# Gate values as two rows spread over the partitions through DRAM, and half of the depthwise convolution on TensorE, in a mixer and mixture-of-experts block

## The chip, the cores and the metric

One core of one Trainium2 chip (trn2) runs the kernel. The metric is the device time of one execution in microseconds (us), median of several runs. The profile is of one execution. TensorE is PE (its weight loads are PEld), VectorE is DVE, ScalarE is ACT, GpSimd is POOL, SyncE is SP.

## The reference, cut to what matters

x has 32 sequences of 256 tokens of width 128. It is normalised, and two branches are added to it: a gated linear recurrence ("mixer") and a mixture of 8 experts with the top 2 of each token.

```python
xn = layernorm(x)
xz = xn @ W_in.T                      # 128 -> 2 x 256
x_proj, z = split(xz)
x_conv = silu(causal_depthwise_conv(x_proj, conv_w, 4 taps) + conv_b)   # per channel, per sequence
x_ssm = x_conv @ W_x.T                # 16 columns Bm, 16 columns Cm, 256 columns dt_in
dt = softplus(dt_in @ W_dt.T + b_dt)
alpha = sigmoid(0.1 * dt)
B_gate = sigmoid(mean(Bm))            # one value per token
C_gate = sigmoid(mean(Cm))            # one value per token
h = scan(clip(alpha, .01, .99), (1 - alpha) * B_gate * x_conv)
y = (h * C_gate + D * x_conv) * silu(z)
out = x + y @ W_out.T + experts(xn)
```

## The kernel before, in words

Channels lie on the partitions (256 of them in two halves, c = 0 and 1) and tokens in the free dimension. A group is 512 tokens, two sequences; there are 16 groups. The program has five stages:

- Setup: x is loaded and normalised, transposed into `xnT`, weights are transposed and folded, the top 2 experts of each token are chosen and each token's row in the expert buffer `moe_in` (DRAM) is worked out.
- Stage A, mixer steps g = 0 to 11. In step g, PE projects and convolves group g+1 and computes for group g; ACT and DVE finish group g-1. At the same time POOL writes token rows to `moe_in` with 128 indirect DMAs (L558), held back by `follow` (L532) to places in DVE's chain.
- Experts: 36 tiles of up to 512 token slots, each with two products, a gate, and a product down (L784 to L841), with inputs loaded by SP. POOL writes the results to `moe_out` (DRAM) with 142 indirect DMAs (L572).
- Steps 12 to 16 of the mixer.
- Sums: as soon as all expert results are written, POOL adds `moe_out` onto `xacc` or the output with 16 accumulating DMAs of 512 KB (L586), blocks 6 and 7 first; SP stores what is finished (L469 to L478).

Each engine's program is written out by hand, in the order of its queue, and semaphores tie the engines. Within one mixer step:

- PE (`mix`, L707): `convolved(g)` (needs the taps of the last step, `s_taps`), `out` (the product with W_out, needs `y2` of DVE), `project` (dt, needs `s_xc` and `s_dt`), `gated` (z), `gates`. `convolved` (L693) projects channel half 1 of both sequences (L694), half 0 of the second sequence (L695), and for half 0 of the first sequence does the convolution itself as four products with pre-scaled weights `Wtap` (L697).
- `gates` (L650) multiplies with `WgB`, whose 128 columns are all equal, so that the mean of Bm (and of Cm) comes out on all 128 partitions: 2 gates x 2 halves of K.
- ACT (`mix`, L988): the first tap with its bias (`acc`, L995 and L1001), silu of the part convolved on PE (L1000), `decay` (tanh `th` L1009, `al` L1015), then a table load (L1025), abs, exp and ln of the softplus (L1030 to L1036), a table load (L1037), silu of z (L1040), tanh of the gates into `thg` (L1044), silu of the rest of the convolution (L1048).
- DVE (`mix`, L1322): taps 1 to 3 (`tap`, L1297: for each, half 0 of the second sequence and half 1 of both), `add_out` (L1319), and the chain: `gbuf` (L1251), clip (L1254), times B gate (L1260), scan (L1266), times C gate (L1271), plus D x (L1277), times silu(z) to `y2` (L1283), and softplus (L1293).
- SP (L418 to L451): when the tables are ready, 8 padding fills of `moe_in` of 266 KB (L420), then stores of finished blocks (`store_base`, L426), then, after `s_xp` 12 and `s_z` 12, the weights of expert tiles 0 and 1 (six DMAs of 128 KB, L436 to L443), then, after all 128 scatters (L444), the rows of tiles 0 and 1 (`xs`, L446).

At the handoff to the experts PE waits for the gates' activation and transposes the rows of tile 0:

```python
            pe.wait_ge(s_thg, STEPS_A)
            transp(0, 0, 0, True)
```

Of the kernel before, what the change touches and what calls it, by code (L numbers as in the profile page):

```python
# [12 lines left out]
P = 128  # L13
# [3 lines left out]
GROUP = 512  # L17
# [43 lines left out]
def block_kernel(nc, x, W_in, conv_w, conv_b, W_x, W_dt, b_dt, A_log, D_skip, W_out,  # L61
                 w_gate, w1, w3, w2, out):
    xs_dram = nc.dram_tensor("moe_in", (EXPERTS * REGION, ROW), F32, kind="Internal").ap()
    yt_dram = nc.dram_tensor("moe_out", (PAIRS, D), F32, kind="Internal").ap()

    ctx = ExitStack()
    with ctx:
# [16 lines left out]
        WgB = sb("WgB", [P, 4, P])  # L84
# [33 lines left out]
        thg = sb("thg", [P, SLOT3, 2, GROUP])  # L118

# [120 lines left out]
        s_tap0 = sem("s_tap0")  # L240
        s_taps = sem("s_taps")
# [11 lines left out]
        s_thg = sem("s_thg")  # L253
        s_ch = sem("s_ch")
# [92 lines left out]
        def _(sp):  # L347
# [70 lines left out]
            sp.wait_ge(s_eid, 1)  # L418
            sp.wait_ge(s_zrow, 1)
            for e in range(EXPERTS):  # L420
# [3 lines left out]
            sp.wait_ge(s_fill, 16 * EXPERTS)  # L424
# [10 lines left out]
            first = []  # L435
            for t in range(2):  # L436
                e = entry(eid_i, t, EXPERTS - 1)
                first.append(entry(src_i, t, EXPERTS * REGION - SLOTS))
# [154 lines left out]
        def _(pe):  # L593
# [56 lines left out]
            def gates(g, slot, b):  # L650
                static = isinstance(g, int)
                if not (static and g < 1):
                    pe.wait_ge(s_thg, g)
# [53 lines left out]
            def mix(g, slot, a, b, c, d):  # L707
                static = isinstance(g, int)
                if a and not (static and g == STEPS_A):
                    if not (static and g + 1 < 1):  # L710
                        pe.wait_ge(s_taps, g + 1)
                    if static and g == 0:
                        pe.wait_ge(s_xc, 1)
                    convolved(g)
                if d:
                    out(g, slot, b)
                if b:
                    project(g, slot, b)
                if a:
# [5 lines left out]
                if b:  # L725
                    if static and g == STEPS_A:
                        pe.wait_ge(s_yc, MOE_TILES)
                    gates(g, slot, b)
# [55 lines left out]
            def up(t, b, first):  # L784
# [3 lines left out]
                for m, (ps, free, done) in enumerate(((PA, s_sil, s_h1), (PB, s_hid, s_h3))):  # L788
                    if not first:
                        pe.wait_ge(free, t)  # L790
                    elif m == 0:
                        pe.wait_ge(s_taps, STEPS_A + 1)
                    else:
# [49 lines left out]
            pe.wait_ge(s_thg, STEPS_A)  # L843
# [47 lines left out]
        def _(act):  # L891
            act.preload_act_table_set("natural_log_exp_and_others")
            def setup(r):
# [7 lines left out]
                elif r == 1:  # L901
# [3 lines left out]
                    act.activation(WgB[:, :, :], PB[:, 512:1024].rearrange("p (a b) -> p a b", a=4),  # L905
# [30 lines left out]
            def take(g):  # L936
# [36 lines left out]
            act.activation(acc[:, 1, :], PA[:, GROUP:2 * GROUP], ACT.Identity, bias=cb[:, 1:2], scale=cw[:, 1, TAPS - 1:TAPS])  # L973
            act.wait_ge(s_xp, 1)
            act.activation(acc[:, 0, SEQ:GROUP], PA[:, SEQ:GROUP], ACT.Identity,
                           bias=cb[:, 0:1], scale=cw[:, 0, TAPS - 1:TAPS]).then_inc(s_tap0, 1)
# [3 lines left out]
            setup(2)  # L980
            act.wait_ge(s_taps, 1)
            act.activation(xc[:, 0, 0, 0:SEQ], PA[:, 0:SEQ], ACT.Silu, bias=cb[:, 0:1])
            act.activation(xc[:, 0].rearrange("p a b -> p (a b)")[:, SEQ:2 * GROUP], flat(acc[:, :, :])[:, SEQ:2 * GROUP],
                           ACT.Silu).then_inc(s_xc, 1)
# [3 lines left out]
            def mix(g, slot, a, b, c, d, held=False):  # L988
                static = isinstance(g, int)
                nxt = (slot + 1) % SLOT3  # L990
                def conv():
                    act.wait_ge(s_xr, g + 2)
                    if not (static and g + 1 < 1):
                        act.wait_ge(s_xc, g + 1)
                    act.activation(acc[:, 1, :], PA[:, GROUP:2 * GROUP], ACT.Identity,  # L995
                                   bias=cb[:, 1:2], scale=cw[:, 1, TAPS - 1:TAPS])
# [3 lines left out]
                    act.activation(xc[:, nxt, 0, 0:SEQ], PA[:, 0:SEQ], ACT.Silu, bias=cb[:, 0:1])  # L1000
                    act.activation(acc[:, 0, SEQ:GROUP], PA[:, SEQ:GROUP], ACT.Identity,  # L1001
                                   bias=cb[:, 0:1], scale=cw[:, 0, TAPS - 1:TAPS]).then_inc(s_tap0, 1)
# [20 lines left out]
                if b:  # L1023
# [13 lines left out]
                    act.preload_act_table_set("silu_and_others")  # L1037
                if a and not held:
                    act.wait_ge(s_z, g + 2)
                    act.activation(sz[:, nxt].rearrange("p a b -> p (a b)"), PB[:, :], ACT.Silu).then_inc(s_sz, 1)  # L1040
                if b:

                    act.wait_ge(s_g, g + 1)
                    act.activation(thg[:, slot].rearrange("p a b -> p (a b)"), PD[:, :], ACT.Tanh,  # L1044
                                   scale=0.5).then_inc(s_thg, 1)
                if a and not held:
                    act.wait_ge(s_taps, g + 2)
                    act.activation(xc[:, nxt].rearrange("p a b -> p (a b)")[:, SEQ:2 * GROUP], flat(acc[:, :, :])[:, SEQ:2 * GROUP],  # L1048
                                   ACT.Silu).then_inc(s_xc, 1)
# [44 lines left out]
            def tile_step(t, n, b, more):  # L1094
# [6 lines left out]
                if more:  # L1101
# [10 lines left out]
            act.activation(xc[:, STEPS_A % SLOT3].rearrange("p a b -> p (a b)")[:, SEQ:2 * GROUP], flat(acc[:, :, :])[:, SEQ:2 * GROUP],  # L1112
                           ACT.Silu).then_inc(s_xc, 1)
# [24 lines left out]
        def _(ve):  # L1138
# [98 lines left out]
            def chain(g, slot, part):  # L1237
# [17 lines left out]
                elif part == 1:  # L1255
# [3 lines left out]
                    ve.wait_ge(s_thg, g)  # L1259
# [37 lines left out]
            def tap(g, j, c_):  # L1297

                if c_ == 0:
                    if j == 1:  # L1300
                        ve.wait_ge(s_tap0, g + 2)
                    else:
                        ve.wait_ge(s_cv, g * 2 + j + 1)
                own = slice(1 - c_, SPG)
                a_v = acc[:, c_, :].rearrange("p (s l) -> p s l", s=SPG)[:, own, j:SEQ]
                p_v = PA[:, c_ * GROUP:(c_ + 1) * GROUP].rearrange("p (s l) -> p s l", s=SPG)[:, own]
                ins = ve.scalar_tensor_tensor(a_v, p_v[:, :, 0:SEQ - j], cw[:, c_, TAPS - 1 - j:TAPS - j],  # L1307
                                              a_v, ALU.mult, ALU.add)
                if c_ == HALVES - 1:
                    ins.then_inc(s_taps if j == TAPS - 1 else s_cv, 1)  # L1310
# [11 lines left out]
            def mix(g, slot, a, b, c, d):  # L1322

                if a:
                    tap(g, 1, 0)
                    tap(g, 1, 1)
# [4 lines left out]
                if a:  # L1331
                    tap(g, 2, 0)
                    tap(g, 2, 1)
                if c:
                    chain(g, slot, 1)
                if a:
                    tap(g, 3, 0)
                    tap(g, 3, 1)
# [7 lines left out]
            def mix_before_experts(g, slot, a, b, c, d):  # L1346


                tap(g, 1, 0)
                tap(g, 1, 1)  # L1350
                add_out(g)
                chain(g, slot, 0)
                for j in (2, 3):
                    tap(g, j, 0)
                    tap(g, j, 1)
# [202 lines left out]
            tap(g, 1, 0)  # L1558
            tap(g, 1, 1)
# [3 lines left out]
            tap(g, 2, 0)  # L1563
            tap(g, 2, 1)
            chain(g, slot, 1)
            tap(g, 3, 0)
            tap(g, 3, 1)
# [9 lines left out]
            tap(g, 1, 0)  # L1577
            tap(g, 1, 1)
            add_out(g)
            chain(g, slot, 0)  # L1580
            tap(g, 2, 0)
            tap(g, 2, 1)
            chain(g, slot, 1)
            tap(g, 3, 0)
            tap(g, 3, 1)
# [55 lines left out]
```

## Time and profile before

| what | value |
|---|---|
| time, median of 3 runs | 488.89 us (488.41 to 489.1) |
| the profiled execution's own time | 488.94 us |
| its span, first to last instruction | 487.0 us |
| busy: PE, DVE, ACT, POOL | 436.2, 410.7, 311.3, 319.6 us |
| DMA traffic | 62.75 MB, 129 GB/s in the mean |
| mean granted clock of PE | 0.974 of full speed |

A share of the span is a mean over stages with different limits, so the rows below are taken stage by stage: what an engine did, and what ended the wait before it ("idle before <- releaser").

### The profile page before, as it was taken

How to read it: one execution, taken by the hardware profiler on the slowest of the kernel's cores; microseconds unless marked ns; L12 is line 12 of the kernel's file. 1: busy time of each engine (PE TensorE's matmuls, PEld its weight loads, DVE VectorE, ACT ScalarE, POOL GpSimd, SP SyncE). 2: the span in 40 equal slices, each digit the busy share in tenths (PEclk: the TensorE clock that was granted, in tenths of full speed). 3: DMA queues.
4: the chain of work that ended last, by engine and by line, in shares of the span. 5: the costliest groups of instructions: out<-in, count | busy, mean ns of one | idle time of the engine just before them, and what ended most of it. 6: DMA issues, size and time to landing. Idle time of an engine off the chain costs nothing. (4 is left out here: it accounts for less than half of the span.)

```text
span 487.0 us, 8269 instructions
## 1 busy us (share of the span) xinstructions
PE 436.2 (90%) x2188; PEld 319.0 (66%) x2188; DVE 410.7 (84%) x868; ACT 311.3 (64%) x421; POOL 319.6 (66%) x345
## 2 busy tenths in 40 slices
PE   0989959899999999998999999999999999999743
PEld 0877525555555555554788888989888999555332
DVE  5999986999999999996997676767777786998993
ACT  2785657888998888898544444444443555698830
POOL 3647777777777777671077777777777777745210
PEclk9999988999999999999999999999999999999876
DMA  9601139122121312132667776666665652039997
GB/s 246 178 3 46 56 101 172 53 66 74 45 93 45 94 45 65 57 111 62 165 190 227 218 219 172 199 179 184 176 186 155 194 173 75 10 50 176 200 212 184
DMA packets 70939, 62.75 MB, mean 129 GB/s; under 512 B 9034, under 2 KB 63214, under 8 KB 70912
## 3 DMA queue, kind: packets, MB, share of 16 engines
q1 hardware_dynamic: 57728, 35.37, 28.0%
q0 software_dynamic: 10944, 25.52, 20.0%
q10 hardware_dynamic: 2240, 1.57, 1.0%
q8 instruction: 9, 0.15, 0.1%
q14 instruction: 18, 0.15, 0.1%
HBM read 38.94 MB, written 29.64 MB: 141 GB/s over the span
## 5 line engine op out<-in xcount | busy, mean ns | idle before, releaser
L572 POOL DMA_INDIRECT moe_out<-xnT,dst_u x142 | 145.5, 1025 | 64.3 <-issue 32.3
L558 POOL DMA_INDIRECT moe_in<-xn,slot_u x128 | 141.5, 1106 | 46.2 <-issue 35.7
L1092 ACT ACTIVATE xn<-PA 128x1024 f32<-128x1024 f32 (+1 forms) x36 | 36.6, 1016 | 61.0 <-PE PA L803 52.3
L1447 DVE TENSOR_TENSOR xn<-xn,PB 128x1024 f32<-128x1024 f32 (+1 forms) x36 | 43.4, 1206 | 33.2 <-PE PB L803 29.3
L837 PE MATMUL PD<-xnT,xn 128*128 128x128 f32 x536 | 65.7, 275 | 0.0
L837 PEld LDWEIGHTS PD<-xnT,xn 128*128 128x128 f32 x536 | 62.8, 192 | 0.0
L685 PE MATMUL PC<-xc,Wc 128*128 128x512 f32 x128 | 59.3, 607 | 2.9 <-DVE ebuf L1293 2.9
L1307 DVE SCALAR_TENSOR_TENSOR acc<-PA,cw,acc 128x255 f32<-128x255 f32 (+2 forms) x96 | 54.2, 606 | 8.2 <-ACT acc L1001 8.1
L658 PE MATMUL PD<-xc,WgB 128*128 128x512 f32 x128 | 57.5, 592 | 0.0
L658 PEld LDWEIGHTS PD<-xc,WgB 128*128 128x128 f32 x128 | 24.2, 190 | 30.1 <-issue 30.1
L672 PE MATMUL PB<-WoT,y 128*128 128x128 f32 x240 | 32.2, 290 | 12.0 <-DVE y L1283 12.0
L685 PEld LDWEIGHTS PC<-xc,Wc 128*128 128x128 f32 x128 | 23.8, 195 | 27.8 <-issue 24.1
L672 PEld LDWEIGHTS PB<-WoT,y 128*128 128x128 f32 x240 | 29.7, 201 | 17.7 <-DVE y L1283 17.2
L1266 DVE TENSOR_TENSOR_SCAN hbuf<-al,gbuf 128x512 f32<-128x512 f32 x32 | 37.3, 1208 | 0.1
L1086 ACT ACTIVATE xhi<-PD 128x512 fp32r<-128x512 f32 (+1 forms) x36 | 21.2, 590 | 24.2 <-PE PD L781 24.2
L697 PE MATMUL PA<-xnT,Wtap 128*128 (+4 forms) x128 | 31.1, 387 | 0.0
L703 PE MATMUL PB<-xnT,WinT 128*128 (+1 forms) x64 | 30.2, 594 | 1.0 <-ACT bdt L912 1.0
L1508 DVE TENSOR_TENSOR xnT<-PD,slot_p 128x512 f32<-128x512 f32 (+1 forms) x36 | 24.6, 683 | 5.9 <-PE PD L837 5.2
L1060 ACT ACTIVATE whi<-xnT 128x512 fp32r<-128x512 f32 x36 | 22.6, 628 | 9.1 <-issue 7.2
L1009 ACT ACTIVATE th<-ebuf,bdt 128x512 f32<-128x512 f32 x32 | 21.3, 714 | 10.8 <-DVE ebuf L1293 10.8
L799 PE MATMUL PA<-xhi,whi 128*128 128x512 f32 x62 | 26.9, 434 | 1.5 <-DVE wlo L1453 0.7
L1030 ACT ACTIVATE ebuf<-PC,bdt 128x512 f32<-128x512 f32 x32 | 20.2, 683 | 11.6 <-PE PC L685 11.6
(211 smaller groups left out, 941.1 us busy)
## 6 DMA issues: line engine op xcount, KB each, us to landing
xnT<-in_L_ffn_w_dram SPq DMA_DIRECT2D x108, 128.0 KB
xn<-moe_in SPq DMA_DIRECT2D x31, 266.0 KB
out_dram<-moe_out POOLq DMA_DIRECT2D x10, 512.0 KB, 15.2
out_dram<-xacc SPq DMA_DIRECT2D x7, 512.0 KB, 3.5
xacc<-moe_out POOLq DMA_DIRECT2D x6, 512.0 KB, 6.7
moe_out<-xnT,dst_u POOLq DMA_INDIRECT x142
moe_in<-zrow SPq DMA_DIRECT2D x8, 266.0 KB, 6.5
moe_in<-xn,slot_u POOLq DMA_INDIRECT x128, 2.4
```

What stands on the lines that cost most here:

```text
L558: gp.indirect_dma_start(xs_dram, bass.IndirectOffsetOnAxis(ap=slot_u[:, k, j:j + 1], axis=0), xn_row[:, j, :], None).then_inc(s_scat, 16)
L572: gp.indirect_dma_start(yt_dram, bass.IndirectOffsetOnAxis(ap=dst_u[:, t, j:j + 1], axis=0), yo[t % OUTS][:, j, :], None, bounds_check=PAI ...
L658: last = pe.matmul(PD[:, n * GROUP:(n + 1) * GROUP], WgB[:, n * 2 + k, :], xc[:, slot, k, :], start=(k == 0), stop=(k == 1))
L672: last = pe.matmul(PB[:, j * D:(j + 1) * D], y2[:, k, j * P:(j + 1) * P], WoT[:, k, :], start=(k == 0), stop=(k == 1))
L685: last = pe.matmul(PC[:, c_ * GROUP:(c_ + 1) * GROUP], Wc[:, k, c_ * P:(c_ + 1) * P], xc[:, slot, k, :], start=(k == 0), stop=(k == 1))
L697: last = pe.matmul(PA[:, j:SEQ], Wtap[:, TAPS - 1 - j, :], source(g, 0, SEQ - j), start=(j == 0), stop=(j == TAPS - 1))
L703: last = pe.matmul(PB[:, c_ * GROUP:(c_ + 1) * GROUP], WinT[:, INNER + c_ * P:INNER + (c_ + 1) * P], source(g), start=True, stop=True)
L837: last = pe.matmul(PD[:, 512 + j * D:512 + (j + 1) * D], hid[b][:, k * SLOTS + j * P:k * SLOTS + (j + 1) * P], (w2x[t - FULL] if mixed and ...
L1092: act.activation(halves(sil, t), halves(PA[:, :], t), ACT.Silu).then_inc(s_sil, 1)
L1266: last = ve.tensor_tensor_scan(hbuf[:, c_, :], al[:, c_, :], gbuf[:, c_, :], 0.0, ALU.mult, ALU.add)
L1307: ins = ve.scalar_tensor_tensor(a_v, p_v[:, :, 0:SEQ - j], cw[:, c_, TAPS - 1 - j:TAPS - j], a_v, ALU.mult, ALU.add)
L1447: ve.tensor_tensor(halves(hid[b], t), halves(sil, t), halves(PB[:, :], t), ALU.mult).then_inc(s_hid, 1)
```

## The change

- `WgB` (128 equal columns) becomes `WgR` with two columns, one for each gate. `gates` then needs two products instead of four and yields two rows of 512 values, on partitions 0 and 1. ACT's tanh works on these two rows (`gt`).
- A new function on SP, `spread_gates(g)`, writes `gt` (4 KB) to the DRAM tensor `gate_rows`, waits until it is written, and reads the row of 1024 values back 128 times, onto every partition of `thg` (512 KB).
- All four taps of channel half 0, of both sequences, are done on PE (`Wtap`); L695, the second `acc` activation and the DVE taps of half 0 go.
- On PE `gates` comes ahead of `gated`; on ACT the tanh of the gates ahead of silu(z).
- On SP the eight fills are no longer one burst: each follows a `spread_gates`, and the stores are put between them. The loads for expert tiles 0 and 1 come behind `spread_gates(11)`. `spread_gates(12)` to `(15)` come behind the expert loads and ahead of the stores.

```diff
+            def spread_gates(g):
+                sp.wait_ge(s_gt, g + 1)
+                if g >= 1:
+                    sp.wait_ge(s_thg, g * 16)
+                if g >= 3:
+                    sp.wait_ge(s_ch, (g - 3) * CHAIN + 6)
+                row = gt_dram[g % SLOT3:g % SLOT3 + 1, :]
+                sp.dma_start(row.rearrange("o (n l) -> (o n) l", n=2), gt[:, :]).then_inc(s_gw, 16)
+                sp.wait_ge(s_gw, (g + 1) * 16)
+                sp.dma_start(thg[:, g % SLOT3].rearrange("p n l -> p (n l)"),
+                             row.broadcast_to([P, 2 * GROUP])).then_inc(s_thg, 16)
...
-            for k in range(STORED - 1):
-                store_base(k)
+            for g in range(STEPS_A - 1):
+                if g >= 4 and g % 2 == 0 and g // 2 - 2 < STORED - 1:
+                    store_base(g // 2 - 2)
+                spread_gates(g)
+                if g < EXPERTS:
+                    fill(g)
+            e01 = [entry(eid_i, t, EXPERTS - 1) for t in range(2)]
+            first = [entry(src_i, t, EXPERTS * REGION - SLOTS) for t in range(2)]
+            spread_gates(STEPS_A - 1)
             sp.wait_ge(s_xp, 12)
             sp.wait_ge(s_z, 12)
...
+            sp.wait_ge(s_fill, 16 * EXPERTS)
             sp.wait_ge(s_scat, 16 * TOP_K * TILES)
...
+            for g in range(STEPS_A, GROUPS):
+                spread_gates(g)
 
             for k in STORES:
...
-                for n in range(2):
-                    for k in range(HALVES):
-                        last = pe.matmul(PD[:, n * GROUP:(n + 1) * GROUP], WgB[:, n * 2 + k, :],
-                                         xc[:, slot, k, :], start=(k == 0), stop=(k == 1))
+                for k in range(HALVES):
+                    last = pe.matmul(PD[0:2, 0:GROUP], WgR[:, k, :], xc[:, slot, k, :], start=(k == 0), stop=(k == 1))
...
-                pe.matmul(PA[:, SEQ:GROUP], WinT[:, 0:P], source(g, SEQ, SEQ), start=True, stop=True)
+                if not (isinstance(g, int) and g + 1 < 1):
+                    pe.wait_ge(s_xq, g + 1)
+                own = PA[:, 0:GROUP].rearrange("p (s l) -> p s l", s=SPG)
+                rows = source(g).rearrange("p (s l) -> p s l", s=SPG)
                 for j in range(TAPS):
-                    last = pe.matmul(PA[:, j:SEQ], Wtap[:, TAPS - 1 - j, :], source(g, 0, SEQ - j),
+                    last = pe.matmul(own[:, :, j:SEQ], Wtap[:, TAPS - 1 - j, :], rows[:, :, 0:SEQ - j],
                                      start=(j == 0), stop=(j == TAPS - 1))
...
-            pe.wait_ge(s_thg, STEPS_A)
+            pe.wait_ge(s_gt, STEPS_A)
...
+                    act.wait_ge(s_g, g + 1)
+                    if not (static and g < 1):
+                        act.wait_ge(s_gw, g * 16)
+                    act.activation(gt[:, :], PD[0:2, 0:GROUP], ACT.Tanh, scale=0.5).then_inc(s_gt, 1)
...
-                    ve.wait_ge(s_thg, g)
+                    ve.wait_ge(s_thg, g * 16)
...
-            def tap(g, j, c_):
+            def tap(g, j):
+                a_v = acc[:, 1, :].rearrange("p (s l) -> p s l", s=SPG)[:, :, j:SEQ]
+                p_v = PA[:, GROUP:2 * GROUP].rearrange("p (s l) -> p s l", s=SPG)
```

## Rows read from the trace of the kernel before

**Rows 1.** Windows by stage: us, each engine's busy time, PEclk, DMA share, GB/s.

```profile
57.00:230.00 173.00, 158.97 (x533) 88.66 (x532) 162.09 (x248) 147.10 (x175) 125.82 (x113) 0.98 0.30 78
230.00:408.00 178.00, 175.99 (x1173) 158.19 (x1173) 134.69 (x298) 82.27 (x116) 127.43 (x125) 1.00 0.64 184
...
433.00:480.00 47.00, 33.77 (x115) 19.86 (x114) 43.30 (x55) 30.33 (x35) 14.11 (x16) 0.84 0.96 179
```

**Rows 2.** Timeline of one step of stage A: start us, us, engine, line, operation.

```profile
160.07 1.22 DVE L1283 TENSOR_TENSOR y<-hbuf,sz 128x1024 f32<-128x1024 f32 x1
...
161.35 2.05 PE L672 MATMUL PB<-WoT,y 128*128 128x128 f32 x16 [0.51 <-DVE y L1283]
...
162.73 1.33 ACT L1009 ACTIVATE th<-ebuf,bdt 128x512 f32<-128x512 f32 x2 [0.84 <-DVE ebuf L1293]
...
164.19 1.22 DVE L1251 SCALAR_TENSOR_TENSOR gbuf<-th,xc 128x1024 f32<-128x1024 f32 x1
...
166.98 1.22 DVE L1260 SCALAR_TENSOR_TENSOR gbuf<-thg,gbuf 128x1024 f32<-128x1024 f32 x1
...
172.55 1.02 ACT L1044 ACTIVATE thg<-PD 128x1024 f32<-128x1024 f32 x1
...
174.23 1.22 DVE L1283 TENSOR_TENSOR y<-hbuf,sz 128x1024 f32<-128x1024 f32 x1
```

**Rows 3.** Timeline, SP's expert loads and the handoff to the experts.

```profile
212.54 0.38 SPq L440 DMA_DIRECT2D xnT<-in_L_ffn_w_dram  x1
...
220.44 0.96 POOL L558 DMA_INDIRECT moe_in<-xn,slot_u  x1 [0.30 <-issue]
...
223.21 0.94 SPq L446 DMA_DIRECT2D xn<-moe_in  x2
...
227.08 1.28 ACT L1037 ACT_TABLE_LOAD   x1
...
228.77 1.02 ACT L1044 ACTIVATE thg<-PD 128x1024 f32<-128x1024 f32 x1 [0.41 <-PE PD L658]
...
229.85 0.66 PE L781 MATMUL PD<-ident,xn 128*128 128x128 f32 x4 [1.11 <-ACT thg L1044]
```

**Rows 4.** Chain that ended last: start us, us, what.

```profile
433.11 5.43 DMA xacc<-moe_out
...
438.83 5.74 DMA xacc<-moe_out
...
444.66 0.69 DVE xacc L1319
...
481.91 0.42 DVE xacc L1612
```

**Rows 5.** DMA queues of 466 to 478 us: packets, MB, share of 16 engines.

```profile
q0 software_dynamic: 677, 2.46, 103.6%
```

**Rows 6.** Timeline of the last step and the last stores.

```profile
464.64 1.02 ACT L1044 ACTIVATE thg<-PD 128x1024 f32<-128x1024 f32 x1 [0.47 <-PE PD L658]
...
470.49 1.22 DVE L1260 SCALAR_TENSOR_TENSOR gbuf<-thg,gbuf 128x1024 f32<-128x1024 f32 x1
...
479.62 1.01 SPq L473 DMA_DIRECT2D out_dram<-xacc  x2
```

**Rows 7.** Windows: tiles 0 and 1 loading; the last stores (columns as rows 1).

```profile
225.00:226.00 1.00, 1.00 (x4) 0.38 (x3) 0.00 (x0) 0.98 (x1) 0.00 (x0) 1.00 1.10 331
...
483.00:484.00 1.00, 0.00 (x0) 0.00 (x0) 0.00 (x0) 0.00 (x0) 0.00 (x0) 1.00 1.03 290
```

**Rows 8.** Groups of instructions: busy us, mean ns, idle before.

```profile
L558 POOL DMA_INDIRECT moe_in<-xn,slot_u x128 | 141.5, 1106 | 46.2 <-issue 35.7 <-DVE hbuf L1266 3.2 <-DVE slot_u L1235 3.0
...
L658 PEld LDWEIGHTS PD<-xc,WgB 128*128 128x128 f32 x128 | 24.2, 190 | 30.1 <-issue 30.1
...
L1307 DVE SCALAR_TENSOR_TENSOR acc<-PA,cw,acc 128x510 f32<-128x510 f32 x16 | 11.8, 738 | 0.0
...
L1307 DVE SCALAR_TENSOR_TENSOR acc<-PA,cw,acc 128x253 f32<-128x253 f32 x16 | 7.6, 476 | 0.1
```

**Rows 9.** DMA issues: KB each, median us to landing.

```profile
out_dram<-xacc SPq DMA_DIRECT2D x7, 512.0 KB, 3.5
```

More of the change, by code:

```diff
@@ L253, in block_kernel @@
         s_thg = sem("s_thg")
+        s_gt = sem("s_gt")
+        s_gw = sem("s_gw")
         s_ch = sem("s_ch")
@@ L416, in load_down, with fill @@
                              w2[bass.ds(e, 1)].rearrange("e (k p) d -> p e k d", p=P)).then_inc(s_w2[b], 16)
-            sp.wait_ge(s_eid, 1)
-            sp.wait_ge(s_zrow, 1)
-            for e in range(EXPERTS):
+            def spread_gates(g):
[9 more added lines that the diff above has]
+                             row.broadcast_to([P, 2 * GROUP])).then_inc(s_thg, 16)
+            def fill(e):
+                if e == 0:
+                    sp.wait_ge(s_eid, 1)
+                    sp.wait_ge(s_zrow, 1)
                 row = entry(pad_i, e, EXPERTS * REGION - SLOTS)
@@ L718, in mix @@
                     project(g, slot, b)
+                    if not (static and g == STEPS_A):
+                        gates(g, slot, b)
                 if a:
@@ L724, in mix @@
                     gated(g)
-                if b:
-                    if static and g == STEPS_A:
-                        pe.wait_ge(s_yc, MOE_TILES)
+                if b and static and g == STEPS_A:
+                    pe.wait_ge(s_yc, MOE_TILES)
                     gates(g, slot, b)
@@ L972, in _ @@
             act.wait_ge(s_xr, 1)
[L973 to L976, printed above, removed]
+            act.activation(acc[:, 1, :], PA[:, GROUP:2 * GROUP], ACT.Identity, bias=cb[:, 1:2],
+                           scale=cw[:, 1, TAPS - 1:TAPS]).then_inc(s_tap0, 1)
             setup(1)
@@ L980, in _ @@
             setup(2)
+            act.wait_ge(s_xp, 1)
+            act.activation(xc[:, 0, 0, :], PA[:, 0:GROUP], ACT.Silu, bias=cb[:, 0:1]).then_inc(s_xq, 1)
             act.wait_ge(s_taps, 1)
-            act.activation(xc[:, 0, 0, 0:SEQ], PA[:, 0:SEQ], ACT.Silu, bias=cb[:, 0:1])
-            act.activation(xc[:, 0].rearrange("p a b -> p (a b)")[:, SEQ:2 * GROUP], flat(acc[:, :, :])[:, SEQ:2 * GROUP],
-                           ACT.Silu).then_inc(s_xc, 1)
+            act.activation(xc[:, 0, 1, :], acc[:, 1, :], ACT.Silu).then_inc(s_xc, 1)
             act.wait_ge(s_z, 1)
@@ L999, in conv @@
                         act.wait_ge(s_ch, g * CHAIN - CHAIN)
[L1000 to L1002 removed]
+                    act.activation(xc[:, nxt, 0, :], PA[:, 0:GROUP], ACT.Silu, bias=cb[:, 0:1]).then_inc(s_xq, 1)
                 def decay():
@@ L1040, in mix @@
                     act.activation(sz[:, nxt].rearrange("p a b -> p (a b)"), PB[:, :], ACT.Silu).then_inc(s_sz, 1)
[L1041 to L1045, printed above, removed]
                 if a and not held:
                     act.wait_ge(s_taps, g + 2)
-                    act.activation(xc[:, nxt].rearrange("p a b -> p (a b)")[:, SEQ:2 * GROUP], flat(acc[:, :, :])[:, SEQ:2 * GROUP],
-                                   ACT.Silu).then_inc(s_xc, 1)
+                    act.activation(xc[:, nxt, 1, :], acc[:, 1, :], ACT.Silu).then_inc(s_xc, 1)
             mixer(act, mix, 0, 1)
@@ L1111, in _ @@
             act.wait_ge(s_taps, held + 2)
-            act.activation(xc[:, STEPS_A % SLOT3].rearrange("p a b -> p (a b)")[:, SEQ:2 * GROUP], flat(acc[:, :, :])[:, SEQ:2 * GROUP],
-                           ACT.Silu).then_inc(s_xc, 1)
+            act.activation(xc[:, STEPS_A % SLOT3, 1, :], acc[:, 1, :], ACT.Silu).then_inc(s_xc, 1)
             gate(0, True)
@@ L1295, in softplus @@
                 last.then_inc(s_dt, 1)
-            def tap(g, j, c_):
[L1299 to L1310, printed above, removed]
+            def tap(g, j):
+                if j == 1:
+                    ve.wait_ge(s_tap0, g + 2)
+                else:
+                    ve.wait_ge(s_cv, g * 2 + j + 1)
+                a_v = acc[:, 1, :].rearrange("p (s l) -> p s l", s=SPG)[:, :, j:SEQ]
+                p_v = PA[:, GROUP:2 * GROUP].rearrange("p (s l) -> p s l", s=SPG)
+                ve.scalar_tensor_tensor(a_v, p_v[:, :, 0:SEQ - j], cw[:, 1, TAPS - 1 - j:TAPS - j],
+                                        a_v, ALU.mult, ALU.add).then_inc(s_taps if j == TAPS - 1 else s_cv, 1)
             def add_out(g):
@@ L1324, in mix @@
                 if a:
-                    tap(g, 1, 0)
-                    tap(g, 1, 1)
+                    tap(g, 1)
                 if d:
@@ L1331, in mix @@
                 if a:
-                    tap(g, 2, 0)
-                    tap(g, 2, 1)
+                    tap(g, 2)
                 if c:
@@ L1336, in mix @@
                 if a:
-                    tap(g, 3, 0)
-                    tap(g, 3, 1)
+                    tap(g, 3)
                 if c:
@@ L1346, in mix_before_experts @@
             def mix_before_experts(g, slot, a, b, c, d):
-                tap(g, 1, 0)
-                tap(g, 1, 1)
+                tap(g, 1)
                 add_out(g)
@@ L1353, in mix_before_experts @@
                 for j in (2, 3):
-                    tap(g, j, 0)
-                    tap(g, j, 1)
+                    tap(g, j)
                 softplus(g)
@@ L1557, in _ @@
             chain(g, slot, 0)
-            tap(g, 1, 0)
-            tap(g, 1, 1)
+            tap(g, 1)
             t = MOE_TILES - 1
@@ L1562, in _ @@
             add_out(g)
-            tap(g, 2, 0)
-            tap(g, 2, 1)
+            tap(g, 2)
             chain(g, slot, 1)
-            tap(g, 3, 0)
-            tap(g, 3, 1)
+            tap(g, 3)
             chain(g, slot, 2)
@@ L1576, in _ @@
             slot = g % SLOT3
-            tap(g, 1, 0)
-            tap(g, 1, 1)
+            tap(g, 1)
             add_out(g)
             chain(g, slot, 0)
-            tap(g, 2, 0)
-            tap(g, 2, 1)
+            tap(g, 2)
             chain(g, slot, 1)
-            tap(g, 3, 0)
-            tap(g, 3, 1)
+            tap(g, 3)
             chain(g, slot, 2)
```

20 lines of the change are left out of this document (10 added, 10 removed).

## The prediction

> **What bounds the kernel now.** I read the windows by stage first [rows 1]. In stage A (57 to 230 us) DVE is busy 162 of 173 us, PE 159, ACT 147. The experts are PE's (176 of 178 us). In the last 47 us DVE is busy 43, and the DMA engines are full (share 0.96). A change to the mixer step can pay in the first and the third stretch, each with its own limit.
>
> The timeline of one step [rows 2] says which wait ends last. From one `y2` (160.07) to the next (174.23) a step takes 14.16 us, and no DVE operation in it has idle time before it. PE is nearly as long: it waits only 0.5 us for `y2`. ACT waits 0.84 us for DVE's softplus before `th`. So DVE bounds stage A, with PE less than 1 us behind.
>
> At the handoff [rows 3] PE waits for ACT's `thg` before it transposes tile 0 at 229.85. The rows of that tile were ordered at 223.21, when POOL's last scatter (220.44) had landed; their weights had been ordered from 212.54 on, 16 us ahead of the last gates.
>
> The chain that ended last [rows 4] shows the tail. DVE's `add_out` of step 14 (444.66) waited for the sums of blocks 6 and 7, which POOL ordered at 433.11, just after its last expert scatter. POOL's scatters follow the experts at their own pace, so the start of the sums moves with the start of the experts. The sums fill the DMA queue until 478 us: in 466 to 478 their queue alone has 103.6% of 16 engines [rows 5], and SP orders the held-back 512 KB stores at 479.62 [rows 6]. The stores run at 290 GB/s [rows 7] to the end at 487. DVE's own last operation is at 481.91 [rows 4]. **Tail = sums plus stores; DVE is a close second.**
>
> **The change, part by part.**
>
> *Gates on PE.* A step of `gates` is 8 passes (128 in 16 steps) at (24.2+30.1)/128 = 0.42 us from start to start [rows 8]. Four go: -1.7 us. The convolution had ten passes of about 255 columns (2.1 us) and gets eight of about 509 (3.4 us): +1.3. PE: -0.4 a step, from 13.6 (14.16 less its wait) to 13.2. I take a pass with 2 weight columns to cost what one with 128 does; were it a quarter cheaper, nothing follows, as PE isn't the bound; were it dearer by 0.2 us, PE would be.
>
> *Taps on DVE.* Three operations of 476 ns [rows 8] go from each step, some 0.39 us each back to back. The first lies ahead of `add_out`: behind it DVE must wait for `th`, which starts at 162.73 and takes 1.33, so L1251 can't start before 164.06, where it stood at 164.19 [rows 2]. That tap gives 0.1, the other two 0.78. A step becomes 14.16-0.88 = 13.3, still just above PE's 13.2. The nine steps from group 2 to 10 give 7.8, and the taps of groups -1 to 1 about 2 (they stand in an unbroken run of DVE, less 0.3 for the longer convolution behind them). The gates of step 11 are ready 9.7 us earlier.
>
> *ACT.* tanh of 2x512 instead of 128x1024 (1.02 us in [rows 2]; `th` does 512 columns in 0.67, so I take 0.6), one `acc` less, `xc` in two pieces of 512: about -0.9 a step. ACT waited before; nothing more follows.
>
> *The trip through DRAM.* New on SP, for each group: a 4 KB write, its landing, a 512 KB read. The nearest row is a 512 KB store, 3.5 us to landing [rows 9], of which 0.52 MB at 290 GB/s [rows 7] are 1.8; so 1.7 are fixed. Trip: 1.7+3.5+0.1 = 5.3 us, from 4.7 (a quicker read) to 8 (scatters in the way, 128 reads of one DRAM row slower). What is there to cover it: the new tanh ends some 1.2 us before `y2`, and L1260 comes 6.9 us after `y2` now [rows 2], 6.4 then. 7.6 against 5.3: hidden, by 2.3.
>
> *SP's order in stage A.* Fills and stores queue behind the trip of their own step and have 8 us to drain before the next. The last scatter, at POOL's 1.47 us apiece ((141.5+46.2)/128, [rows 8]), comes some 5 us sooner, its landing at 218.
>
> *The handoff, where the gain is lost.* Tile 0's and 1's six weight loads and both loads of rows now stand behind `spread_gates(11)`. The tanh of step 11 would end at 227.08+1.28+0.6-9.7 = 219.3 [rows 3]. Written at 221.2; then the read and six loads are ordered at 0.47 each (two in 0.94 now [rows 3]), so the rows of tile 0 at 224.5, later than the 223.21 of now. Before them 0.5+0.8 MB stand in the same queue, with them 1.55 MB, from 222.6 on (223.21 ordered, full at 225 now): at 290 GB/s [rows 7] until 227.9. PE transposes at 227.95 instead of 229.85: **-1.9 us** remain of 9.7. Bounds: -2.5 (at the 331 GB/s that the rows of tiles 0 and 1 reach now [rows 7]) to +1.5 (trip of 7).
>
> *Steps 12 to 14.* PE reaches `out` and `project` of step 12 some 1.2 us later, since the convolution stands ahead of them; ACT and DVE save about as much. `add_out` of step 14 waits for the sums anyway [rows 4], so nothing ahead of it counts.
>
> *The tail.* The trips of groups 13, 14 and 15 fall between 437 and 473, where the engines are full. Cost of their 3x512 KB to the sums: nothing if they fit in gaps, 3x1.8 = 5.4 if they add at the stores' rate. The queue's 103.6% [rows 5] is nearest to adding; the loads of the handoff show reads at 331 GB/s where stores reach 290 [rows 7], 1.6 us for 512 KB, so I take 1.5 each: **+4.5 us**. The sum chain: 479.62-1.9+4.5 = 482.2, and 7.4 from there to the end of the span: 489.6. The DVE chain: the last tanh (464.64) gives gates for 470.49 [rows 6]; that is 4.8 us from the end of today's tanh at 465.66, and about 5.7 from that of the new one, against a trip of 7 to 9 under full engines: +1.5 to +3, so its last operation is near 482.5, behind the stores that run until 489. The Trainium skill ("DMA: Bandwidth & Descriptors", section on queues, rings and completion order) has each DMA engine take turns between queues packet by packet: by that rule each read takes turns with the sums, 1.8 us become 3.6, and the sums pay all of it, 5.4. The same page's section on latency gives HBM 0.2 us in the mean and 2 us at high load; by it the last trip would be 2 us longer still. No row of before has a plain read beside the sums.
>
> **Sum:** the profiled execution is 488.94 (span 487.0 plus 1.94), and the median of the runs is 488.89, so no correction. 488.94-1.9+4.5 = **491.5 us**.
>
> **Rivals.**
>
> - *The trips vanish in the sums' gaps* (faster): a sum reads two places and writes one, and a plain read may run while an engine waits for its own. For: the sums move only 2.46 MB in 12 us, 205 GB/s, where stores reach 290 [rows 5, 7]. Against: [rows 5]. Then 488.94-1.9 = 487.0; 20%.
> - *All of stage A's gain arrives* (faster): the loads behind `spread_gates(11)` are no limit. Then POOL's scatters would be: landed at 218 instead of 223, rows 3.5 us later, start near 221.6: 488.94-8.3+4.5 = 485, or 481 with the tail absorbed. Against: the order of SP's queue; 6%.
> - *The trip is longer than its cover* (slower than forecast): it decides from 7.6 us. At 9 us DVE waits at L1260 for about 0.7 us in each of ten steps, the gain of stage A falls from 9.7 to near 3, and the rows of tile 0 come 6 to 7 us later than forecast: 498. For: scatters take 30% of the engines [rows 1], and all 128 reads go to one row of DRAM. 22%.
> - The forecast itself, between 488.5 and 494: 52%.
>
> **How the numbers follow.** About 0.2% (1 us) can be told from no change. Faster by more: the first rival mostly (0.16), the second (0.06), and an edge of the forecast (0.03): 0.25. Within 0.2%: 0.17. Slower: 0.58. The range must hold 8 in 10: from 485.5 (first rival with its bounds) to 498 (the third).
>
> **What would show it.** In the changed profile: steps of stage A at 13.3; L1260 with no wait in them (a wait there is the third rival); the tanh of step 11 near 219 and PE and DVE idle from then to about 228, released by the rows of tile 0; sums that start near 431.2 and take some 4 us more; a wait for the trip at L1260 in the last step; the stores after 482. The prediction is wrong if PE starts the experts before 224, if the step is over 14, or if the sums take no longer than 46 us.

## The result, and the profile after

Before: 489.6 us (median of 11 runs beside the changed kernel, 488.41 to 490.56). Changed: **493.29 us** (11 runs, 490.48 to 496.26), a ratio of 1.0072 with a 95% interval of 1.005 to 1.0094. That is slower by 0.7%, clear of the 0.2% that can be told apart. In a later set the ratio was 1.0107 (1.0088 to 1.0127). The profiled execution took 491.32 us, its span 489.4: 2.4 us above the profile of before, where the medians are 3.7 apart.

The windows by stage of the changed kernel, columns as in [rows 1]:

```profile
57.00:230.00 173.00, 157.47 (x475) 70.03 (x474) 150.23 (x215) 140.13 (x167) 115.55 (x113) 0.96 0.39 116
230.00:408.00 178.00, 177.10 (x1177) 159.02 (x1176) 132.86 (x296) 81.74 (x113) 128.40 (x127) 1.00 0.64 183
433.00:480.00 47.00, 27.64 (x90) 14.15 (x88) 37.28 (x45) 27.79 (x33) 12.20 (x14) 0.79 1.02 210
```

Against [rows 1], DVE is busy 12 us less up to 230 and 6 us less in the tail, though the kernel is slower. The taps that went are work that DVE no longer has; where the time went instead, the rows below must say. The DMA engines go from 0.96 to 1.02 in the tail. Now one step of stage A, from the timeline, beside [rows 2]:

```profile
136.25 0.59 ACT L1065 ACTIVATE gt<-PD 2x512 f32<-2x512 f32 x1
...
138.07 1.22 DVE L1304 TENSOR_TENSOR y<-hbuf,sz 128x1024 f32<-128x1024 f32 x1
...
139.34 2.05 PE L696 MATMUL PB<-WoT,y 128*128 128x128 f32 x16
...
141.57 0.69 DVE L1335 TENSOR_TENSOR xacc<-PB,xacc 128x512 f32 x1 [0.31 <-PE PB L696]
...
144.58 1.22 DVE L1281 SCALAR_TENSOR_TENSOR gbuf<-thg,gbuf 128x1024 f32<-128x1024 f32 x1
...
149.62 0.59 ACT L1065 ACTIVATE gt<-PD 2x512 f32<-2x512 f32 x1
...
151.44 1.22 DVE L1304 TENSOR_TENSOR y<-hbuf,sz 128x1024 f32<-128x1024 f32 x1
```

From `y2` to `y2` it is 13.37 us instead of 14.16. PE's `out` still starts 0.05 us behind the end of `y2`, in every step, and `add_out` (L1335) waits 0.31 us for it. Before, `add_out` needed no wait, but it stood equally far behind `y2`: 3.51 us there (from 160.07 in [rows 2] to the line below), 3.50 here.

```profile
163.58 0.69 DVE L1319 TENSOR_TENSOR xacc<-PB,xacc 128x512 f32 x1
```

So the step is a circle through both engines: `y2`, PE's `out`, `add_out`, DVE's chain to the next `y2`. PE's own passes need about 12.9 us of the 13.37 (an estimate: 26 passes of 0.43 us from start to start, and 16 of `out` at 0.11). L1281, which needs the gates that came through DRAM, has no idle time before it. The previous tanh ended at 136.84, so the trip (its read landed after 4.1 us in the median) had 7.7 us.

The handoff, from the timeline, beside [rows 3]:

```profile
216.52 0.59 ACT L1065 ACTIVATE gt<-PD 2x512 f32<-2x512 f32 x1
217.13 0.28 SPq L430 DMA_DIRECT2D gate_rows<-gt  x1
218.34 0.32 SPq L432 DMA_DIRECT2D thg<-gate_rows  x1
218.91 0.35 SPq L462 DMA_DIRECT2D xnT<-in_L_ffn_w_dram  x1
...
221.92 0.94 SPq L469 DMA_DIRECT2D xn<-moe_in  x2
...
226.40 1.09 PE L807 MATMUL PD<-ident,xn 128*128 128x128 f32 x4 [10.95 <-DMA xn<-moe_in]
...
228.78 0.63 PE L827 MATMUL PA<-xhi,wlo 128*128 128x512 f32 x1
...
231.34 0.43 PE L827 MATMUL PB<-xhi,wlo 128*128 128x512 f32 x1
...
430.33 1.91 POOL L612 DMA_DIRECT2D xacc<-moe_out  x2 [1.89 <-issue]
```

The tanh of step 11 is done at 217.11, 12.7 us ahead of before (229.79). PE stands still for 10.95 us until the rows of tile 0 are there, and starts 3.45 us ahead of before. It starts at the lower clock: the granted clock is 0.50 in 226 to 230, and a pass shows 0.63 us, then 0.43 from 231.3. POOL orders the sums at 430.33, 2.8 us ahead of before.

The tail, from the chain that ended last, beside [rows 4]:

```profile
436.34 2.24 DMA gate_rows<-gt
438.60 7.79 DMA thg<-gate_rows
...
446.42 1.23 DVE gbuf L1281
...
462.76 4.40 DMA gate_rows<-gt
467.18 8.09 DMA thg<-gate_rows
...
475.29 1.24 DVE gbuf L1281
...
486.72 0.42 DVE xacc L1617
```

Before, no trip stood in this chain. Beside the sums a write takes 2.2 to 4.6 us and a read about 8, where stage A shows 1.2 and 4.1. DVE waits for the gates of groups 13, 14 and 15: 1.36, 4.70 and 1.96 us, 8.0 in all. Its last operation is at 486.72 instead of 481.91. The longest of these waits and SP's stores, from the timeline, beside [rows 6]:

```profile
462.25 1.22 DVE L1281 SCALAR_TENSOR_TENSOR gbuf<-thg,gbuf 128x1024 f32<-128x1024 f32 x1 [4.70 <-DMA thg<-gate_rows]
...
481.15 1.01 SPq L499 DMA_DIRECT2D out_dram<-xacc  x2
```

From the order of the sums to this line it is 50.8 us; before, 46.5. The whole: the sums start 2.8 earlier and take 4.3 longer. DVE ends 4.8 later, and the last small store waits for it, so that the span ends 8.25 us behind this line and not 7.4. -2.8+4.3+0.9 = 2.4, the difference of the two spans.

### The profile page after: what moved, and what is told of

It reads as the page before. It is cut to its first block, busy times and chain, and to the rows that moved or that the text cites. A ratio compares the mean times of both kernels' runs of the same rounds, so it can differ in the third digit from the quotient of the medians.

```text
span 489.4 us, 8075 instructions
## 1 busy us (share of the span) xinstructions
PE 431.0 (88%) x2092; PEld 291.0 (59%) x2092; DVE 392.7 (80%) x820; ACT 298.0 (61%) x405; POOL 308.1 (63%) x345
## 4 chain that ended last, share of the span: by engine, by line
PE 72%; DVE 14%; DMA 7%; ACT 3%; issue 3%; SPq 1%; DVEq 0%
PE PD L864 13%; PE PC L709 10%; PE PA L724 9%; PE PB L696 5%; PE PB L730 4%; PE PD L683 4%; DMA thg<-gate_rows 3%; PE PD L807 3%; PE PA L830 3%; PE PA L826 3%; PE PA L827 3%; PE PB L826 3%; PE PB L830 3%; PE PB L827 3%; PE PA L718 2%
## 5 line engine op out<-in xcount | busy, mean ns | idle before, releaser
L584 POOL DMA_INDIRECT moe_in<-xn,slot_u x128 | 131.3, 1026 | 44.6 <-issue 37.9
L724 PE MATMUL PA<-xnT,Wtap 128*128 (+4 forms) x128 | 57.2, 590 | 0.0
L724 PEld LDWEIGHTS PA<-xnT,Wtap 128*128 128x128 f32 x128 | 24.3, 190 | 30.5 <-issue 30.5
L1325 DVE SCALAR_TENSOR_TENSOR acc<-PA,cw,acc 128x510 f32<-128x510 f32 (+2 forms) x48 | 35.5, 739 | 1.5 <-ACT acc L1020 1.3
L730 PE MATMUL PB<-xnT,WinT 128*128 (+1 forms) x64 | 31.6, 617 | 1.0 <-ACT bdt L939 1.0
L807 PE MATMUL PD<-ident,xn 128*128 128x128 f32 x142 | 21.8, 276 | 11.0 <-DMA xn<-moe_in 11.0
L683 PE MATMUL PD<-xc,WgR 128*2 128x512 f32 x64 | 30.0, 592 | 0.0
```

The source lines that it names most:

```text
L584: gp.indirect_dma_start(xs_dram, bass.IndirectOffsetOnAxis(ap=slot_u[:, k, j:j + 1], axis=0), xn_row[:, j, :], None).then_inc(s_scat, 16)
L683: last = pe.matmul(PD[0:2, 0:GROUP], WgR[:, k, :], xc[:, slot, k, :], start=(k == 0), stop=(k == 1))
L724: last = pe.matmul(own[:, :, j:SEQ], Wtap[:, TAPS - 1 - j, :], rows[:, :, 0:SEQ - j], start=(j == 0), stop=(j == TAPS - 1))
L730: last = pe.matmul(PB[:, c_ * GROUP:(c_ + 1) * GROUP], WinT[:, INNER + c_ * P:INNER + (c_ + 1) * P], source(g), start=True, stop=True)
```

## The experiments

**Theory:** stage A gains about 10 us and loses them at two places, the order of SP's queue at the handoff and the trips beside the sums. **Rivals:** POOL, the fills or the clock hold the experts back; the tail is longer by the convolution on PE; the trip is too long for stage A.

**Loads first.** The trip of group 11 behind the loads of tiles 0 and 1. Its gates are needed only after the experts have begun.

```diff
-            spread_gates(STEPS_A - 1)
             sp.wait_ge(s_xp, 12)
...
             for t in range(2):
                 sp.dma_start(xs[t], ...)
+            spread_gates(STEPS_A - 1)
```

> The six weight loads and both loads of rows of tiles 0 and 1 stand ahead of the trip of group 11 on SyncE; nothing else differs from the changed kernel. Theory (the gain of stage A is lost in SyncE's order at the handoff): rows of tile 0 are ordered when the last scatter has landed, near 211, PE transposes them as soon as the tanh of step 11 is done, near 217.2 instead of 226.4, and the sums start near 421 instead of 430.3: about 484 us. Rival (something other than these loads holds the experts back: the fills, POOL, the clock of TensorE): transposes stay near 226 and the time near 493.

Measured: **482.27 us** (479.18 to 484.48), 0.9835 of before (0.981 to 0.986). Its timeline:

```profile
213.94 0.94 SPq L468 DMA_DIRECT2D xn<-moe_in  x2
...
218.26 0.59 ACT L1065 ACTIVATE gt<-PD 2x512 f32<-2x512 f32 x1
...
218.90 0.66 PE L807 MATMUL PD<-ident,xn 128*128 128x128 f32 x4 [1.71 <-ACT gt L1065]
```

PE starts tile 0 behind the tanh, with 1.71 us of idle time instead of 10.95, and the sums are ordered at 423.01. One moved line is worth 11.0 us of the medians. The two profiled executions are 6.8 us apart (484.48, the slowest of this kernel's six, and 491.32), and the sums 7.3. The start of stage A took 1.7 us longer in this one, a difference between executions (last section), so some 9 us of the 11.0 can be seen in the traces. POOL, the fills and the trips of stage A are as in the changed kernel, so none of them held the experts back.

**Weights first.** Only the six weight loads ahead; the rows stay behind the trip.

```diff
-            spread_gates(STEPS_A - 1)
             sp.wait_ge(s_xp, 12)
...
+            spread_gates(STEPS_A - 1)
             sp.wait_ge(s_fill, 16 * EXPERTS)
```

> The six weight loads of tiles 0 and 1 ahead of the trip of group 11, both loads of rows still behind it. It splits the handoff's loss between weights and rows. Theory: rows ordered 3 us sooner and with no weights in the queue ahead of them, so transposes some 4.5 us earlier than in the changed kernel (near 222): about 489 us; the remaining half of the gain of having all loads early belongs to the rows. Rival (only the rows count, as the queue has room for both): near 493.

This kernel, the two halves of the change and the kernel with two reads (below) ran in two sets on two other chips, on which the kernel before took 561.85 and 561.41 us, 15% more. Instructions lasted the same there (592 ns a pass), but more time went into waits, some of which the profile calls remote: from `y2` to `y2` across the experts it is 232 to 235 us, and 176 in the changed kernel. The changed kernel did not run there, and the forecasts in us were made for the faster chips, so these kernels are read by intervals of their traces. The time was 569.84 us, 1.0102 of before (1.0032 to 1.0172), so 489 and 493 can't be told apart by it. The timeline:

```profile
243.64 0.29 SPq L430 DMA_DIRECT2D gate_rows<-gt  x1
...
245.43 0.97 SPq L469 DMA_DIRECT2D xn<-moe_in  x2
...
250.27 1.08 PE L807 MATMUL PD<-ident,xn 128*128 128x128 f32 x4 [8.32 <-DMA xn<-moe_in]
```

From the write of the last gates to PE's transposes it is 6.6 us. It is 9.3 in the changed kernel, 8.9 to 9.5 in the other six profiles that kept its order (9.5 in both of this kernel's own set), and 0.0 with all loads first. So the weights made 2.3 to 2.9 us of it (4.5 were expected), and the rows behind the trip the larger part.

**Local gates in the tail.** Groups 12 to 15 as before: replicated weights kept beside the two-column ones, tanh straight into `thg`.

```diff
-            for g in range(STEPS_A, GROUPS):
-                spread_gates(g)
...
+                if local:
+                    for n in range(2):
+                        for k in range(HALVES):
+                            last = pe.matmul(PD[:, n * GROUP:(n + 1) * GROUP], WgB[:, n * 2 + k, :], ...)
...
+                    if local:
+                        act.activation(thg[:, slot]..., PD[:, :], ACT.Tanh, scale=0.5).then_inc(s_gt, 1)
```

> Groups 12 to 15 get their gates as before the change (eight passes with replicated weights, tanh of 128x1024 straight into thg), so no trip runs in the tail; stage A and the handoff are those of the changed kernel. Theory (the three trips beside the sums cost the tail about 5 us, by the reads' bandwidth and by DVE's waits): the sums take about 46.5 us again instead of 50.8, no wait at the gated product, last DVE operation near 480: about 488 us. Rival (the tail is longer because of the convolution on TensorE at a low clock): stays near 493.

Measured: 489.63 us (487.05 to 491.76), 0.999 of before (0.997 to 1.001), 3.7 under the changed kernel. The timeline, SP and DVE:

```profile
473.48 1.22 DVE L1299 SCALAR_TENSOR_TENSOR gbuf<-thg,gbuf 128x1024 f32<-128x1024 f32 x1
...
480.25 1.02 SPq L498 DMA_DIRECT2D out_dram<-xacc  x2
...
484.89 0.42 DVE L1635 TENSOR_TENSOR xacc<-PB,xacc 128x256 f32<-128x256 f32 x1 [1.28 <-PE PB L919]
```

Sums ordered at 433.05, stores at 480.25: 47.2, close to the 46.5 of before. There is no wait for gates; but DVE's last operation is still 51.8 us behind the sums' order (48.8 before; 50.1 in the three other profiles with local gates, below), not near 480. Here the chain runs through PE: its four extra passes a step are back while the longer convolution stays, and `add_out` of step 14 waits 1.49 us for PE. So the rival has a part, which the trips had covered.

**Local gates, reads kept.** The reads of 512 KB are still made, into memory that nobody reads.

```diff
+            for g in range(STEPS_A, GROUPS):
+                sp.wait_ge(s_gt, g + 1)
...
+                sp.dma_start(xnT[:, spent:spent + 2 * GROUP], row.broadcast_to([P, 2 * GROUP])).then_inc(s_thg, 16)
```

> As the kernel with local gates in the tail, and SyncE still issues a 512 KB replicated read of a row of gates for each of groups 12 to 15, into memory that nothing reads; no operation waits for them. It measures the bandwidth of the reads apart from DVE's waits. Prediction's step (1.5 us for each of three reads beside the sums): sums end 4.5 us later than with local gates alone, time near 492. Rival (the reads fit in the sums' gaps, and only the waits cost): equal to the kernel with local gates alone, near 488.

Measured: 491.56 us (489.51 to 493.02), 1.0036 of before (1.002 to 1.0051): 1.9 us above local gates alone, with intervals that don't touch, and 1.7 below the changed kernel. DMA issues of 431 to 481 us, and the timeline of SP:

```profile
xnT<-gate_rows SPq DMA_DIRECT2D x3, 512.0 KB, 8.1
```

```profile
481.00 1.01 SPq L504 DMA_DIRECT2D out_dram<-xacc  x2
```

Ordered at 431.06, so 49.9 us for the sums, 2.7 more than without the reads: **0.9 us a read** on the sums, not 1.5. The two profiles of the next kernel, which has no reads either, show 48.2 and 47.0 us, so it is between 0.6 and 1.0; the 1.9 us of the medians are 0.6 a read. While a read runs the queues together move 249 to 298 GB/s, and 210 without one, so part of a read seems to fit beside the sums. The other 1.7 us, up to the changed kernel, come with the writes and with DVE's waits, which no run tells apart.

**Both edits.**

> Both edits of the two other kernels: loads of tiles 0 and 1 ahead of the trip of group 11, and gates of groups 12 to 15 without a trip. Theory: the two losses lie one behind the other and add, so about 479 us, faster than before by 2%. Rival (an earlier end of the experts meets another limit, such as DVE in the tail): above 484.

Measured: 477.99 us (474.79 to 481.33), 0.9741 of before (0.9714 to 0.9768). The two losses add: 11.0 and 3.7 alone, 15.3 together. The profiles are only 10.0 apart (481.33, the slowest of this kernel's six, and 491.32); up to 3.1 of the rest is the start of stage A, early in the one and late in the other (last section), and at least 2 us are not traced. Then again beside the changed kernel, on one chip:

> The changed kernel itself, as the yardstick for the kernels that ran on the chip on which the kernel of before takes 561 us. Theory: its ratio to before lies near 1.007 again, a little above if waits there cost more; the kernel with the weights first (1.010) then lies within the noise of it and the kernel with two reads (1.029) clearly above. Rival (on that chip the change costs far more than 0.7%): above 1.02, and the ratios of the others must be read against that.

> The kernel with the loads of tiles 0 and 1 ahead of the trip of group 11 and local gates in the tail, beside the changed kernel on the same chip. Theory: the two edits take away what they took on the first chip, 3.1% of the time of the changed kernel, so about 0.98 to 0.985 of before. Rival (the gain hangs on the first chip): at or above before.

This set fell on a chip on which before takes 489.46 us, so it is no yardstick for the slower ones. It repeats the first result: changed 494.37 us (1.0107), both edits **476.81 us**, 0.9736 (0.9715 to 0.9757). Against the changed kernel that is 0.9736/1.0107 = 0.963, more than the 3.1% that were expected to go, and below the forecast of 0.98 to 0.985 of before. In the profile of the changed kernel the sums are ordered at 430.12, the stores at 479.66 (49.5 us, where the first profile had 50.8), and DVE waits 8.2 us for the tail's gates, in the same three places.

**Half of the change alone.** Convolution only (gates, tanh and SP of before), and gates only (convolution and taps of before), each once on each of the two slower chips.

```diff
-                pe.wait_ge(s_gt, STEPS_A)
+                pe.wait_ge(s_thg, STEPS_A)
...
+                        last = pe.matmul(PD[:, n * GROUP:(n + 1) * GROUP], WgB[:, n * 2 + k, :], ...)
```

```diff
-                ve.scalar_tensor_tensor(a_v, p_v[:, :, 0:SEQ - j], cw[:, 1, ...], ...)
+                    tap(g, 1, 0)
+                    tap(g, 1, 1)
```

> Only the convolution's half of the change: gates, tanh, SyncE's order and the fills are those of before. Theory (with the convolution on TensorE, TensorE bounds a step, and it is the four passes of the gates that make room for it): a step of stage A is 13.38 us plus four passes of 0.43, about 15.1 instead of 14.16, so the ten steps lose some 8 and the start gains some 3: about 496 us. Rival (VectorE bounds the step and the three taps are what counts): steps near 13.4, the handoff as before with the loads early, about 481.

> The kernel with only the convolution's half of the change, again, since the four kernels of its first set ran on a chip on which every kernel took some 15% longer. There TensorE's passes stood back to back at 14.64 us a step. Theory: 14.64 instead of 14.16 bounds stage A, ten steps lose some 5 and the start gains some 3, the handoff and the tail are those of before: about 492 us. Rival (VectorE's taps count): about 481.

> Only the gates' half: two-row gates, the trips, SyncE's order and the spread fills, with the convolution of before. Theory: the step stays at 14.16 us by VectorE, so stage A gains only the earlier tanh (about 1.5 us); the loads behind the trip of group 11 cost the handoff some 6 us and the tail's trips some 4: about 499 us. Rival (TensorE's shorter step speeds stage A by itself): steps under 13.8 and the time below 495.

> The kernel with only the gates' half, again, for the same reason. Theory: VectorE holds the step at 14.16 us, the gates of step 11 come about 1.5 us earlier than before, the loads behind the trip of group 11 make the handoff some 6 us later than before, the tail's trips cost some 4: about 499 us. Rival (the spread fills or the shorter TensorE step give something back): below 495.

Measured, as ratios to before in the same set: convolution 1.0108 (1.0064 to 1.0151) and 1.0197 (1.0142 to 1.0252), gates 1.0362 (1.0306 to 1.0418) and 1.0415 (1.0357 to 1.0472). One kernel differs by 0.9% between the two sets, so such a ratio is not to be read more closely than that. The absolute forecasts can't be judged there. The timeline of PE, convolution only, second run:

```profile
193.63 1.02 PE L697 MATMUL PA<-xnT,WinT 128*128 x2
194.49 3.58 PE L703 MATMUL PA<-xnT,Wtap 128*128 x8
...
204.84 3.60 PE L661 MATMUL PD<-xc,WgB 128*128 128x512 f32 x8
208.28 1.02 PE L697 MATMUL PA<-xnT,WinT 128*128 x2
```

PE's passes stand back to back at 14.65 us a step, above the 14.16 of before. My first figure, 15.1, was too high: it took the 13.38 of the changed kernel for PE's own length. 14.65 less four passes of 0.43 is 12.9, so in the changed kernel PE has some 0.4 us to spare. The same trace shows the circle through both engines at work. Where PE is not late for `y2`, the step is 13.38 us here too, though PE has four passes more:

```profile
152.60 1.22 DVE L1282 TENSOR_TENSOR y<-hbuf,sz 128x1024 f32<-128x1024 f32 x1
...
153.88 2.05 PE L675 MATMUL PB<-WoT,y 128*128 128x128 f32 x16 [0.30 <-issue]
...
156.10 0.69 DVE L1313 TENSOR_TENSOR xacc<-PB,xacc 128x512 f32 x1 [0.30 <-issue]
...
165.98 1.22 DVE L1282 TENSOR_TENSOR y<-hbuf,sz 128x1024 f32<-128x1024 f32 x1
```

In the next step PE comes to `out` 1.42 us behind the end of `y2`, and DVE waits. With gates only, 10 of 18 steps are 14.15 to 14.35, DVE's length; the others are longer. Neither half shortens the step, so each bears only its own cost: the step falls because DVE's taps go and PE's gate passes make room for them.

**Two reads.** In groups 0 to 10 the read is made twice, one behind the other.

```diff
+                if g < STEPS_A - 1:
+                    sp.dma_start(thg[:, g % SLOT3]..., row.broadcast_to([P, 2 * GROUP])).then_inc(s_first, 16)
+                    sp.wait_ge(s_first, (g + 1) * 16)
```

> The changed kernel, and in groups 0 to 10 the 512 KB read is made twice, the second behind the landing of the first, so that a trip takes about 9.4 us instead of 5.3. It tests the prediction's cover of 7.6 us and its third rival. Theory (the trip and what follows it until the next tanh are a circle): each step grows by what exceeds 7.7 us, about 1.7, to 15.0; waits at the gated product in ten steps; about 508 us. Rival (VectorE's slack takes it up): steps near 13.4 and 493.

Measured on the first of the slower chips: 579.88 us, 1.0288 (1.0236 to 1.034). The timeline of DVE:

```profile
160.38 1.23 DVE L1286 SCALAR_TENSOR_TENSOR gbuf<-thg,gbuf 128x1024 f32<-128x1024 f32 x1 [1.81 <-DMA thg<-gate_rows]
...
173.86 1.22 DVE L1286 SCALAR_TENSOR_TENSOR gbuf<-thg,gbuf 128x1024 f32<-128x1024 f32 x1
...
188.79 1.23 DVE L1286 SCALAR_TENSOR_TENSOR gbuf<-thg,gbuf 128x1024 f32<-128x1024 f32 x1 [1.46 <-DMA thg<-gate_rows]
```

The wait that is absent in the changed kernel is there, in five steps of ten. In the first row the write had been ordered at 150.75, 9.6 us earlier; less the wait of 1.81 that is 7.8 us of cover, the 7.6 of the prediction. Nine steps take 130.1 us, 14.46 each, against 13.38 in the undisturbed ones: +1.1 a step, where 1.7 was expected. Not all of it is the second read: the waits at this line add to 7.3 us in these steps, 0.8 each, and the kernel with the weights first, with one read, takes 13.85 a step on this chip. A step with the wait is followed by one without, so not all of the excess is paid each time.

## Why the prediction was right, point by point

Sign and the two places of the loss came as forecast, and the time lies in the range (491.5 for a median of 493.3), but several terms were off and one step was wrong. That the forecast lies within 0.2 us of the profiled execution (491.32) is in part luck: the handoff kept 0.9 us more than forecast, and DVE's late end cost 0.9 that was not in the sum. The median lies 2 us above that execution, and this part of the result is not in the trace that is read here.

- **PE and DVE in a step.** Forecast 13.3 by DVE with PE at 13.2; measured 13.37, by DVE and the `out` that it waits for, with PE's passes at 12.9. The first tap gave 0.01 us and the other two 0.78 (0.1 and 0.78 forecast). What stands behind the first tap is `add_out`, which must wait for `out`; the prediction named `th`. A pass with two weight columns took 592 ns, as one with 128 does, as was assumed.
- **Stage A.** Nine steps gave 7.6 us (7.8 forecast). The start gave 4.3 and not 2, and in this execution some 3 of it is the clock (below). The tanh of step 11 ended at 217.1, not 219.3.
- **The trip.** Write 1.2 and read 4.1 us, 5.3 in all as forecast, and no wait in stage A. The parts were forecast as 1.7 and 3.5, so the sum came out by two errors that cancel. The rival of the long trip (22%) fell.
- **The handoff.** The mechanism is shown by the loads-first kernel. The rows were ordered at 221.9 and there at 226.3, 1.6 earlier than forecast. The tanh was 2.2 earlier and the write 0.7 shorter, but from the order of the read to the rows it took 8.0 us and not 6.7. PE started 3.45 us ahead of before; at the sums 2.8 were kept and not 1.9, as the lower clock behind PE's idle time took back part. The rival with 6%, the whole gain arriving, was priced at 485: that is what the kernel becomes (482.3) once the loads are no limit.
- **The sums.** Term +4.5, measured +4.3 and, in the second profile, +3.0, but only in part for the reason given: the reads alone cost 0.6 to 1.0 each, 1.8 to 3.0. What lengthened the sums by the rest (the writes, or `add_out` of step 14 at another time) was not separated.
- **The step that failed** is "DVE chain +1.5 to +3 by late gates of the last step, behind the stores". I priced a trip under full engines at 7 to 9 us and only for the last group. It takes 10.1, 12.6 and 12.5 us, and all three are waited for: 8.0 us. DVE ends at 486.7, not 482.5, and sets the end together with the stores. The Trainium skill ("DMA: Bandwidth & Descriptors", sections on queues, rings and completion order and on latency) has each DMA engine take turns between queues packet by packet, and HBM's latency grow under load. The trace agrees in direction: reads go from 4.1 to about 8 us, writes from 1.2 to 2.2 in one case and 4.4 and 4.6 in the others. The prediction applied this to DVE's wait for the last trip alone, where it bore on all three.

## What to carry to other kernels

When a step gets a new wait on a queue that other work uses in order, ask of each thing behind it how early it could have gone: here one moved line was worth 11 us, three times what the change cost. A round trip that is hidden in one stage must be costed again in each stage in which the engines are full, once per group. Two edits of which neither shortens a step alone can do so together; here the two engines stood within 1 us of each other. An engine that shows no idle time need not be the one that sets the step: its number of passes, times what one takes, says what it needs.

## What the runs showed of the hardware that was not expected

The clock of PE at the start of stage A. The timelines of PE in the kernel before, in the changed kernel and in the one with both edits (its first run):

```profile
70.96 2.07 PE L694 MATMUL PA<-xnT,WinT 128*128 128x512 f32 x2 [5.73 <-DVE acc L1307]
```

```profile
68.75 1.12 PE L718 MATMUL PA<-xnT,WinT 128*128 128x512 f32 x2 [2.74 <-DVE acc L1325]
69.71 3.58 PE L724 MATMUL PA<-xnT,Wtap 128*128 128x512 f32 x8
```

```profile
68.77 2.07 PE L724 MATMUL PA<-xnT,WinT 128*128 128x512 f32 x2 [2.75 <-DVE acc L1343]
70.64 5.74 PE L730 MATMUL PA<-xnT,Wtap 128*128 128x512 f32 x8
```

Before, PE waits 5.73 us for the taps and then runs at the lower level: two passes last 2.07 us. The changed kernel waits 2.74 us, and in its two profiles (and in the one with the reads kept) the granted clock stays at 1.00: that is most of the gain at the start that I had not counted. After the same wait the kernel with both edits fell to 0.52 in both its profiles, and eight passes took 5.74 us instead of 3.58. The `y2` of step 1 came at 84.5 to 84.7 us in three traces, at 86.1 to 86.3 in two and at 87.6 in two. The kernel with the loads first, whose code up to there is that of the changed one, is among those at 86.3. (The kernels with local gates have one more copy on ACT ahead of it.) So executions differ here by 1.7 us with the same code, and by up to 3.1 over all seven; the changed kernel's runs spread over 5.8 us and those of before over 2.1. What decides it stays open.
